# A two-layer GNN on one core: early zeros, and a packed copy of layer 1's edge rows

## The chip, the cores and the metric

The kernel runs on one core of a Trainium2 chip. The metric is the device time of one execution in microseconds (us). Engines are named as in the profile: PE (TensorE), DVE (VectorE), ACT (ScalarE), POOL (GpSimd) and SP (SyncE, which here only issues DMAs). Each engine runs its own program in order, and they meet at semaphores.

## The reference

There are 6250 nodes and 206250 edges (100000 random pairs in both directions, and a self loop each), sorted by destination. Both layers take the same edges. Cut to what matters:

```
for layer, attr, kd in ((0, edge_attr_16, 16), (1, edge_attr_64, 64)):
    h = relu(layernorm(x))                       # 6250 x 64
    if layer == 0:
        ea  = attr @ W_edge.T + b_edge
        agg = segment_sum(relu(h[src] + ea), dst)
        g   = (h + agg) @ W1.T + b1
        g   = relu(batch_norm(g, gamma, beta)) @ W2.T + b2
    else:
        y   = relu(concat(h[src], attr) @ M_W.T + M_b)
        z   = segment_sum(y, dst)
        g   = relu(concat(h, z) @ U_W.T + U_b)
    x = x + g
```

## The kernel before

The edges are cut into 34 groups (NB) of 31 tiles of 128 edges whose order is changed, and 16 "plain" tiles, and a 35th part of plain tiles alone. A turn works on one group. Layer 0 has 33 turns after a first group, and so has layer 1. Two sets of buffers alternate.

**The edge store.** PE projects the attributes of an edge for both layers at once (line 1128), ACT takes the results out of PSUM (lines 862 and 865) into a staging row of 132 floats (528 B), and POOL scatters the rows of one tile of 128 edges to their slots in DRAM with one indirect DMA (line 732). A group has 6400 slots (50 columns of 128), sorted by source node. The first 66 floats of a row are layer 0's half, those from 64 on are layer 1's half (they share two floats of metadata). Slots that no edge takes must be zero, so `fill` (line 523) writes 3300 KB of zeros before a group is scattered, three groups ahead of its use. Layer 0 reads its half of a group with `load_edges` (line 527), layer 1 reads the other half with `load_edges_part` (line 532) in two parts; both take one run of 264 B from each row: 6400 runs in a group, 4096 and 2304 in the two parts.

**A turn.** Edges of a group are met with node rows by one-hot matmuls on PE (lines 1163, 1181), added and passed through relu on DVE and ACT (lines 1600, 907), and summed by destination in a window with another one-hot matmul (line 1193; DVE line 1591 makes the one-hot). Layer 0 also makes the one-hot matrix of the sources (DVE 1576) and SP stores it (line 546, `store_src`), from where layer 1 loads it on ACT's queue (line 912). For plain tiles POOL gathers node rows with 16 indirect DMAs in a turn (line 754), in both layers.

**The order of the work** is written out by hand: every engine's program is a loop over turns, with two turns in its body. SP's in layer 0 is `turn`, which walks over u = 0 to 6: `store_src` at each, `next_edges` (line 527) at u = 1, attributes (line 473) at u = 2, 4, 5, 6, the zeros of the group three ahead at u = 3, plain indices at u = 4; then attributes of the next plain tiles and the plain rows (line 515). A DMA that waits for a semaphore holds up all that follow it on SP. POOL scatters 16 tiles, later 15, and gathers 16 in one turn of layer 0. In layer 1 `turn_l1` issues indices, the two parts of an edge load two groups ahead, and plain rows (line 519).

**Before the loops** SP issues attributes for group 0, the zeros of group 0, indices, the rest of group 0's attributes, x, four attribute loads of group 1, the zeros of group 1, and so on (lines 586 to 627). `load_first` from the third on waits for a projection. DVE makes layernorm steps (lines 1405 to 1442) and POOL's slot indices (line 1531), and adds b2 to x (line 1772) ahead of the first group. At the end of each layer every engine waits for a flag and loads it into a register (line 460, in `if_general`), to decide whether a general path for unusual graphs is needed; it isn't with these inputs.

Of the kernel before, what the change touches and what calls it, by code (L numbers as in the profile page):

```python
# [212 lines left out]
def build(nc, x, idx, dst, attr0, attr1, params, out):  # L213
# [4 lines left out]
    store_groups = store.rearrange("(g r) c -> g r c", r=GROUP_ROWS)  # L218
    plain_store = nc.dram_tensor("plain_store", (PARTS, P, PLAIN * D), F32, kind="Internal").ap()
    src_store = nc.dram_tensor("src_store", (NB, NODE_P, NODE_COLS * P), BF16, kind="Internal").ap()  # L220
    with ExitStack() as ctx:
# [185 lines left out]
        rows_landed = [[sem(f"rows_landed{s}_{v}") for v in range(NV)] for s in range(2)]  # L407
        plain_projected = sem("plain_projected")
# [48 lines left out]
        def if_general(eng, general):  # L457

            eng.wait_ge(windows_ready, 1)
            more = eng.value_load(flag_int[0:1, 0:1], min_val=0, max_val=1)  # L460
            with eng.If(more > 0):
                general()
                eng.nop()
            with eng.Else():
                eng.nop()
            eng.nop()

        @block.sync
        def _(sp):
# [60 lines left out]
            def load_edges_part(g, p, k):  # L530
                j, nj = LOAD_PARTS[k]
                sp.dma_start(edge[p][:, j:j + nj, :], store_groups[bass.ds(g, 1), 0:CAP * NODE_COLS, D:D + HALF_ROW]
                             .rearrange("a (p j) c -> p (a j) c", j=NODE_COLS)[:, j:j + nj, :]).then_inc(dense_sems[1].e_landed[p], 16)
# [53 lines left out]
            sp.dma_start(dst_all[:, 0:head], dst[:, 0:head]).then_inc(head_landed, 16)  # L587
            for quarter in range(2):
                load_first(0, quarter)
            sp.wait_ge(memsets_done, 1)  # L590
            fill(0, 0)
# [8 lines left out]
            for quarter in range(NQ):  # L600
                load_first(1, quarter)
            fill(1, 1)
            sp.wait_ge(filled[0], 16)
# [21 lines left out]
            for u in range(NU):  # L625
                store_src(0, 0, u)

# [7 lines left out]
            def turn(n, s, more=True, more_fill=True):  # L635

                m = n * 2 + s
                for u in range(NU):
                    store_src(m + 1, 1 - s, u)
                    if u == 1 and not (isinstance(m, int) and m + 2 >= NB):  # L640
                        next_edges(m, s)
                    if more and u in (2, 4, 5, 6):
                        load(m, (2, 4, 5, 6).index(u) + 2)
                    if u == 4:
                        next_plain_idx(0, n, s)
                    if u == 3 and more and more_fill:
# [16 lines left out]
            if_general(sp, lambda: general(0))  # L663

            sp.wait_ge(dense_sems[0].rows_used, NB * NU + 2)
            for g in range(2):
                for k in range(2):
                    load_edges_part(g, g, k)
# [45 lines left out]
            if_general(sp, lambda: general(1))  # L714
# [7 lines left out]
        def _(pool):  # L722
# [61 lines left out]
            if_general(pool, lambda: general(0))  # L784
# [14 lines left out]
            if_general(pool, lambda: general(1))  # L799

        @block.scalar
        def _(act):
# [235 lines left out]
            for m in range(LAST_PREPARED, NB - 1):  # L1038
                dense_turn(0, m // 2, m % 2, more=m <= LAST_PREPARED, last=m == NB - 2, bank=0)
            for m in range(NB - 1, PARTS):  # L1040
                last_plain(0, m)
            last_windows(0)
            if_general(act, lambda: general(0))
# [30 lines left out]
            for m in range(NB - 4, NB - 1):  # L1074
                dense_turn(1, m // 2, m % 2, last=m == NB - 2)
            for m in range(NB - 1, PARTS):
                last_plain(1, m)
            last_windows(1)
            if_general(act, lambda: general(1))

        @block.tensor
        def _(pe):
# [263 lines left out]
            for m in range(LAST_PREPARED + 1, NB - 1):  # L1346
                dense_turn(0, m // 2, m % 2, last=m == NB - 2, bank=0)
            for m in range(NB - 1, PARTS):
                last_plain(0, m)
            last_windows(0)  # L1350
            if_general(pe, lambda: general(0))
# [25 lines left out]
            dense_turn(1, (NB - 2) // 2, 0, last=True)  # L1377
            for m in range(NB - 1, PARTS):
                last_plain(1, m)
            last_windows(1)  # L1380
            if_general(pe, lambda: general(1))
# [10 lines left out]
        def _(dve):  # L1392
# [356 lines left out]
            for step in range(NG + 3):  # L1749
# [17 lines left out]
                if step == 5:  # L1767
# [18 lines left out]
            for m in range(LAST_PREPARED + 1, NB - 1):  # L1786
                dense_turn(0, m // 2, m % 2, last=m == NB - 2)
            for m in range(NB - 1, PARTS):
                last_plain(0, m)
            last_windows(0)  # L1790
            if_general(dve, lambda: general(0))
# [52 lines left out]
            dense_turn(1, (NB - 2) // 2, 0, last=True)  # L1844
            for m in range(NB - 1, PARTS):
                last_plain(1, m)
            last_windows(1)
            if_general(dve, lambda: general(1))
# [76 lines left out]
```

## Time and profile before

| | us |
|---|---|
| median of 3 runs | 4705.78 |
| lowest, highest | 4699.32, 4708.74 |
| profiled execution | 4683.44 |
| its span, first to last instruction | 4681.6 |
| POOL busy, instructions | 2085.3, 2185 |
| PE busy, instructions | 2569.9, 25733 |
| mean granted clock of PE, share of full speed | 0.673 |

Busy time is time in which an engine runs an instruction; registers, branches and DMA issues don't count. In a timeline a row gives start, length, what ran, and in brackets how long the engine was idle before and what released it: "issue" means that it waited for nothing that the profile shows, "remote" or "an unknown queue" that the releaser is not known. A "q" after an engine's name is its sequencer. For SP the length of a row of several issues reaches from the first to the last.

### The profile page before, as it was taken

How to read it: one execution, taken by the hardware profiler on the slowest of the kernel's cores; microseconds unless marked ns; L12 is line 12 of the kernel's file. 1: busy time of each engine (PE TensorE's matmuls, PEld its weight loads, DVE VectorE, ACT ScalarE, POOL GpSimd, SP SyncE). 2: the span in 40 equal slices, each digit the busy share in tenths (PEclk: the TensorE clock that was granted, in tenths of full speed). 3: DMA queues.
4: the chain of work that ended last, by engine and by line, in shares of the span. 5: the costliest groups of instructions: out<-in, count | busy, mean ns of one | idle time of the engine just before them, and what ended most of it. 6: DMA issues, size and time to landing. Idle time of an engine off the chain costs nothing. (4 is left out here: it accounts for less than half of the span.)

```text
span 4681.6 us, 73575 instructions
## 1 busy us (share of the span) xinstructions
PE 2569.9 (55%) x25733; PEld 2124.4 (45%) x25733; DVE 1518.7 (32%) x2605; ACT 961.3 (21%) x2153; POOL 2085.3 (45%) x2185
## 2 busy tenths in 40 slices
PE   3455546554655556555456554655655545555554
PEld 3454445444544445444445444544544434443443
DVE  4422223222332223322232222322444434433443
ACT  1322212211221112221122221212321111111111
POOL 4444444455345543454434444354244443444343
PEclk9766667666666666766666666666667666666676
DMA  6554435443444434544345444443355555555552
GB/s 191 142 140 124 114 106 144 135 116 106 123 132 135 112 105 123 136 132 113 106 129 141 118 113 112 123 118 81 93 123 126 122 120 116 125 121 121 115 123 55
DMA packets 703632, 565.17 MB, mean 121 GB/s; under 512 B 491942, under 2 KB 605748, under 8 KB 699042
## 3 DMA queue, kind: packets, MB, share of 16 engines
q1 hardware_dynamic: 625244, 402.10, 34.3%
q0 software_dynamic: 69440, 107.94, 9.1%
q10 hardware_dynamic: 8736, 51.91, 3.2%
q8 instruction: 180, 2.95, 0.3%
q14 instruction: 32, 0.26, 0.0%
HBM read 294.89 MB, written 266.88 MB: 120 GB/s over the span
## 5 line engine op out<-in xcount | busy, mean ns | idle before, releaser
L1193 PE MATMUL ps_w<-arena 128*64 128x128 f32 (+1 forms) x9040 | 1209.1, 313 | 1031.1 <-issue 942.3
L732 POOL DMA_INDIRECT edge_store<-side,slot_idx x1054 | 1018.3, 966 | 1544.0 <-issue 1244.5
L754 POOL DMA_INDIRECT gathered_rows<-node_table_l,plain_slot x1116 | 1059.2, 949 | 957.9 <-DVE arena L1614 573.1
L1193 PEld LDWEIGHTS ps_w<-arena 128*64 128x64 f32 x9040 | 898.8, 165 | 1235.4 <-issue 1119.5
L1591 DVE TENSOR_TENSOR arena<-ps_c,dst_rel 128x1024 f32<-128x1024 f32 (+1 forms) x476 | 526.1, 1105 | 1186.4 <-remote 890.6
L907 ACT ACTIVATE arena<-arena 128x512 f32<-128x512 f32 (+1 forms) x616 | 366.2, 595 | 2369.3 <-remote 887.3
L1128 PE MATMUL ps_p<-w_both,side 80*128 80x128 f32 x3228 | 647.1, 362 | 368.1 <-issue 109.6
L1128 PEld LDWEIGHTS ps_p<-w_both,side 80*128 80x128 f32 x3228 | 565.4, 262 | 419.4 <-issue 245.5
L1600 DVE TENSOR_TENSOR arena<-ps_r,arena 128x512 f32<-128x512 f32 (+1 forms) x476 | 299.4, 629 | 586.0 <-remote 562.8
L1576 DVE TENSOR_SCALAR arena<-arena,iota_p 125x512 bf16<-125x512 bf16 (+1 forms) x442 | 147.5, 351 | 940.7 <-ACT arena L894 538.6
L1181 PE MATMUL ps_r<-tab,arena 125*128 125x64 bf16 x5100 | 287.6, 213 | 251.2 <-issue 132.7
L1181 PEld LDWEIGHTS ps_r<-tab,arena 125*128 125x128 bf16 x5100 | 238.8, 111 | 324.6 <-issue 248.7
L894 ACT ACTIVATE arena<-ps_b 125x512 bf16<-125x512 f32 (+1 forms) x442 | 244.2, 575 | 520.7 <-remote 474.2
L862 ACT ACTIVATE side<-ps_p 128x512 f32<-128x512 f32 (+1 forms) x272 | 156.9, 577 | 516.0 <-remote 346.5
L1181 PE MATMUL ps_r<-tab,ranking 125*128 125x64 bf16 x2550 | 139.0, 209 | 166.7 <-issue 161.1
L1163 PE MATMUL ps_b<-ident_b,marks_b 128*125 128x128 bf16 x1700 | 214.9, 263 | 22.1 <-ACT dst_rel L888 17.0
L1181 PE MATMUL ps_r<-tab,side 125*128 125x64 bf16 x2550 | 135.4, 206 | 156.0 <-issue 155.7
L1181 PEld LDWEIGHTS ps_r<-tab,ranking 125*128 125x128 bf16 x2550 | 107.9, 108 | 208.9 <-issue 201.1
L1181 PEld LDWEIGHTS ps_r<-tab,side 125*128 125x128 bf16 x2550 | 104.9, 106 | 195.2 <-issue 189.1
L1163 PEld LDWEIGHTS ps_b<-ident_b,marks_b 128*125 128x125 bf16 x1700 | 168.9, 171 | 24.5 <-issue 23.1
L1591 DVE TENSOR_TENSOR arena<-ps_c,plain_rel 128x576 f32<-128x576 f32 x140 | 105.2, 752 | 52.2 <-remote 38.1
L874 ACT ACTIVATE plain_e<-ps_p 128x512 f32<-128x512 f32 x140 | 79.9, 592 | 192.4 <-remote 145.6
(124 smaller groups left out, 1026.3 us busy)
## 6 DMA issues: line engine op xcount, KB each, us to landing
edge_store<-zeros SPq DMA_DIRECT2D x34, 3300.0 KB
arena<-edge_store SPq DMA_DIRECT2D x34, 1650.0 KB
src_store<-arena SPq DMA_DIRECT2D x204, 250.0 KB
side<-attr SPq DMA_DIRECT2D x172, 256.0 KB
arena<-edge_store SPq DMA_DIRECT2D x34, 1056.0 KB
arena<-edge_store SPq DMA_DIRECT2D x34, 594.0 KB
plain_store<-plain_e SPq DMA_DIRECT2D x35, 512.0 KB
side<-plain_store SPq DMA_DIRECT2D x35, 512.0 KB
```

The lines of the kernel that those rows point to most:

```text
L732: pool.indirect_dma_start(out=store, in_=stage[:, c, i, :], in_offset=None, out_offset=bass.IndirectOffsetOnAxis(ap=slot_idx[:, s, t + i:t ...
L754: pool.indirect_dma_start(out=rows[s][:, i, :], out_offset=None, in_=table[layer], in_offset=bass.IndirectOffsetOnAxis(ap=plain_slot[:, s, ...
L862: act.activation(stage[:, c, 0:nt, :].rearrange("p t (l r) -> p t l r", l=2)[:, :, :, 0:D], ps_p[(s + 1 + c) % 2][:, 0:nt * P].rearrange(" ...
L894: act.activation(spread_src[0:NODE_P, (p + i // 2) % 2, i % 2, 0:nt * P], ps_b[(p + i) % 2][0:NODE_P, 0:nt * P], ACT.Copy).then_inc(copied, 1)
L907: act.activation(msg[:, slot, 0:nt, :], pre[:, slot, 0:nt, :], ACT.Relu).then_inc(d.relu_done, 1)
L1128: last = pe.matmul(ps_p[bank][:, i * P:(i + 1) * P], attr_buf[:, slot, e:e + P], w_both[:, :], start=True, stop=True)
L1163: last = pe.matmul(ps_b[(p + i) % 2][0:NODE_P, t * P:(t + 1) * P], marks_b[:, p, j + t:j + t + 1].broadcast_to([P, NODE_P]), ident_b[:, :] ...
L1181: last = pe.matmul(ps_r[slot][:, to:to + D], match, tab[:, j + t, k, :], start=(k == 0), stop=(k == 2))
L1193: mm = pe.matmul(ps_sum[layer][t % 2][:, 0:width], msg[:, slot, t, :], dst_match[:, slot, t, 0:width], start=(first and t <= layer), stop= ...
L1576: dve.tensor_scalar(src_match[0:NODE_P, slot, i % 2, 0:nt * P], spread_src[0:NODE_P, slot, i % 2, 0:nt * P], iota_p[0:NODE_P, 1:2], None, ...
L1591: dve.tensor_tensor(dst_match[:, slot, 0:nt, 0:width], iota[:, 0:width].unsqueeze(1).broadcast_to([P, nt, width]), rel.unsqueeze(2).broadc ...
L1600: dve.tensor_tensor(pre[:, slot, 0:nt, :], ps_r[(p + u) % 2][:, 0:nt * D].rearrange("p (t d) -> p t d", d=D), edge[p][:, j:j + nt, at:at + ...
```

## The change

- A second DRAM tensor, `e1_store`, holds layer 1's half of every row of a group side by side, per partition. In each turn of layer 0 for which group m + 2 exists, SP copies that half from `edge_store` with one DRAM to DRAM DMA, at u = 5 behind the attribute load; groups 0 and 1 are copied before the first turn. Layer 1 waits once for all copies and loads from there: per partition one run of 8448 B and one of 4752 B.
- In the prologue the zeros of group 0 go before the first attribute loads, and those of group 1 after two instead of four attribute loads of that group.
- DVE's addition of b2 moves from before the first group to after the first two turns.
- PE, ACT and DVE load the flag before their last plain units instead of after them. SP and POOL load it where they did.

```diff
+    e1_store = nc.dram_tensor("e1_store", (NB, P, NODE_COLS * HALF_ROW), F32, kind="Internal").ap()
...
-        def if_general(eng, general):
-
+        def general_flag(eng):
             eng.wait_ge(windows_ready, 1)
-            more = eng.value_load(flag_int[0:1, 0:1], min_val=0, max_val=1)
+            return eng.value_load(flag_int[0:1, 0:1], min_val=0, max_val=1)
+
+        def if_general(eng, more, general):
+
             with eng.If(more > 0):
...
             def load_edges_part(g, p, k):
                 j, nj = LOAD_PARTS[k]
-                sp.dma_start(edge[p][:, j:j + nj, :], store_groups[bass.ds(g, 1), 0:CAP * NODE_COLS, D:D + HALF_ROW]
-                             .rearrange("a (p j) c -> p (a j) c", j=NODE_COLS)[:, j:j + nj, :]).then_inc(dense_sems[1].e_landed[p], 16)
+                sp.dma_start(edge[p][:, j:j + nj, :].rearrange("p j c -> p (j c)"),
+                             e1_store[bass.ds(g, 1), :, j * HALF_ROW:(j + nj) * HALF_ROW].rearrange("a p c -> (a p) c"))\
+                    .then_inc(dense_sems[1].e_landed[p], 16)
+
+            def pack_e1(g):
+
+                sp.dma_start(e1_store[bass.ds(g, 1)].rearrange("a p (j c) -> p (a j) c", c=HALF_ROW),
+                             store_groups[bass.ds(g, 1), 0:CAP * NODE_COLS, D:D + HALF_ROW]
+                             .rearrange("a (p j) c -> p (a j) c", j=NODE_COLS)).then_inc(e1_packed, 16)
...
+            sp.wait_ge(memsets_done, 1)
+            fill(0, 0)
             for quarter in range(2):
                 load_first(0, quarter)
-            sp.wait_ge(memsets_done, 1)
-            fill(0, 0)
...
-            for quarter in range(NQ):
+            for quarter in range(2):
                 load_first(1, quarter)
             fill(1, 1)
+            for quarter in range(2, NQ):
+                load_first(1, quarter)
...
             for u in range(NU):
                 store_src(0, 0, u)
+            for g in range(2):
+                pack_e1(g)
...
                     if u == 4:
                         next_plain_idx(0, n, s)
+                    if u == 5 and not (isinstance(m, int) and m + 2 >= NB):
+                        pack_e1(m + 2)
...
             sp.wait_ge(dense_sems[0].rows_used, NB * NU + 2)
+            sp.wait_ge(e1_packed, NB * 16)
             for g in range(2):
                 for k in range(2):
                     load_edges_part(g, g, k)
...
+            more = general_flag(act)
             for m in range(NB - 1, PARTS):
                 last_plain(0, m)
             last_windows(0)
-            if_general(act, lambda: general(0))
+            if_general(act, more, lambda: general(0))
...
-            dve.wait_ge(centred[0], NG)
-            dve.tensor_tensor(xs[:, :, :], xs[:, :, :],
-                              prm("b2", NODE_P).unsqueeze(1).broadcast_to([NODE_P, NODE_COLS, D]), ALU.add)\
-                .then_inc(b2_added, 1)
...
             for s in range(2):
                 dense_turn(0, 0, s, more=True, first=s == 0)
+            dve.wait_ge(centred[0], NG)
+            dve.tensor_tensor(xs[:, :, :], xs[:, :, :],
+                              prm("b2", NODE_P).unsqueeze(1).broadcast_to([NODE_P, NODE_COLS, D]), ALU.add)\
+                .then_inc(b2_added, 1)
```

The flag's lines stand alike for both layers and for PE and DVE.

## Rows read from the trace of the kernel before

**Rows 1.** The page, part 1: busy time and share of each engine.

```profile
PE 2569.9 (55%) x25733; PEld 2124.4 (45%) x25733; DVE 1518.7 (32%) x2605; ACT 961.3 (21%) x2153; POOL 2085.3 (45%) x2185
```

**Rows 2.** Timeline of POOL, a turn of layer 0: start, length, what, [idle <- releaser].

```profile
1882.54 1.00 POOL L732 DMA_INDIRECT edge_store<-side,slot_idx  x1 [31.55 <-issue]
...
1908.88 0.96 POOL L732 DMA_INDIRECT edge_store<-side,slot_idx  x1 [6.34 <-ACT side L865]
```

**Rows 3.** Timeline of PE in the same turn, columns as before.

```profile
1925.95 0.46 PE L1193 MATMUL ps_w<-arena 128*64 128x128 f32 x1 [1.04 <-issue]
...
1953.30 3.78 PE L1128 MATMUL ps_p<-w_both,side 80*128 80x128 f32 x16 [5.29 <-ACT plain_e L874]
```

**Rows 4.** Windows of that turn: busy PE, PEld, DVE, ACT, POOL; PEclk, DMA share, GB/s.

```profile
1867.00:1877.00 10.00, 7.04 (x121) 6.30 (x118) 9.57 (x22) 4.11 (x10) 0.00 (x0) 1.00 1.04 204
1881.00:1897.00 16.00, 8.18 (x78) 6.46 (x76) 3.26 (x7) 2.40 (x6) 11.11 (x12) 0.89 0.95 296
...
1912.00:1947.00 35.00, 12.82 (x68) 8.84 (x67) 1.85 (x3) 2.11 (x6) 26.47 (x29) 0.60 0.19 48
```

**Rows 5.** Windows of layer 1, same columns; the last three are turns.

```profile
3912.00:3932.00 20.00, 6.69 (x87) 4.43 (x83) 3.60 (x5) 2.00 (x5) 15.12 (x16) 0.64 0.61 158
4581.00:4596.00 15.00, 12.51 (x187) 10.78 (x188) 10.62 (x15) 3.77 (x8) 0.00 (x0) 0.70 0.01 2
4488.20:4525.20 37.00, 20.49 (x293) 15.73 (x289) 14.63 (x21) 6.11 (x14) 15.13 (x17) 0.68 0.52 120
4525.20:4560.80 35.60, 18.61 (x292) 14.89 (x289) 14.48 (x21) 6.04 (x14) 15.10 (x17) 0.71 0.55 117
...
4596.90:4631.00 34.10, 19.44 (x276) 14.49 (x272) 14.42 (x21) 6.12 (x14) 15.12 (x16) 0.70 0.14 32
```

**Rows 6.** Chain of waits of layer 1: start, length, what.

```profile
4490.32 3.54 another core or an unknown queue
4493.94 16.92 another core or an unknown queue
```

**Rows 7.** Timeline of SP (its DMA issues), turns of layer 0.

```profile
1867.13 0.63 SPq L527 DMA_DIRECT2D arena<-edge_store  x1
1870.09 5.28 SPq L546 DMA_DIRECT2D src_store<-arena  x1
...
1907.97 1.06 SPq L473 DMA_DIRECT2D side<-attr  x2
...
1920.13 38.77 SPq L473 DMA_DIRECT2D side<-attr  x6
...
1965.25 0.64 SPq L527 DMA_DIRECT2D arena<-edge_store  x1
```

**Rows 8.** Timeline of SP in a turn of layer 1.

```profile
3905.34 18.83 SPq L532 DMA_DIRECT2D arena<-edge_store  x2
```

**Rows 9.** Line 532, issue ns min/median/max, first and last start.

```profile
L532 SPq DMA_DIRECT2D arena<-edge_store x68: 378/384/17404, 3345.6 to 4559.2; - x68
```

**Rows 10.** Timeline of POOL in the prologue.

```profile
85.98 0.96 POOL L732 DMA_INDIRECT edge_store<-side,slot_idx  x1 [26.69 <-DMA edge_store<-zeros]
...
132.59 0.96 POOL L732 DMA_INDIRECT edge_store<-side,slot_idx  x1 [5.90 <-ACT side L865]
```

**Rows 11.** Timeline of SP in the prologue.

```profile
42.39 0.87 SPq L473 DMA_DIRECT2D side<-attr  x2
...
68.25 4.28 SPq L473 DMA_DIRECT2D side<-attr  x4
72.57 6.73 SPq L523 DMA_DIRECT2D edge_store<-zeros  x2
```

**Rows 12.** Timeline of DVE in the prologue.

```profile
116.04 1.77 DVE L1517 TENSOR_TENSOR ranking<-ps_p,ranking 128x1550 f32<-128x1550 f32 x1 [9.70 <-remote]
...
154.48 3.49 DVE L1772 TENSOR_TENSOR xs<-xs,par 125x3200 f32<-125x3200 f32 x1
```

**Rows 13.** Timeline of DVE between the layers.

```profile
3353.27 3.00 DVE L1797 BATCH_NORM_STATS2 bn<-acc 64x6 f32<-64x500 f32 x5 [1.20 <-DVEq L1792]
```

More of the change, by code:

```diff
@@ L407, in build @@
         rows_landed = [[sem(f"rows_landed{s}_{v}") for v in range(NV)] for s in range(2)]
+        e1_packed = sem("e1_packed")
         plain_projected = sem("plain_projected")
@@ L662, in _ @@
                 store_plain(m)
-            if_general(sp, lambda: general(0))
+            if_general(sp, general_flag(sp), lambda: general(0))
             sp.wait_ge(dense_sems[0].rows_used, NB * NU + 2)
+            sp.wait_ge(e1_packed, NB * 16)
             for g in range(2):
@@ L713, in _ @@
                 turn_l1(m // 2, m % 2, more=m < NB - 3)
-            if_general(sp, lambda: general(1))
+            if_general(sp, general_flag(sp), lambda: general(1))
             for g, (j, m) in enumerate(GROUPS):
@@ L782, in general @@
                             ).then_inc(e.rows_landed, 16)
-            if_general(pool, lambda: general(0))
+            if_general(pool, general_flag(pool), lambda: general(0))
             pool.wait_ge(turned[0], NG)
@@ L798, in _ @@
             gather_plain(1, NB // 2, 0)
-            if_general(pool, lambda: general(1))
+            if_general(pool, general_flag(pool), lambda: general(1))
         @block.scalar
@@ L1075, in _ @@
                 dense_turn(1, m // 2, m % 2, last=m == NB - 2)
+            more = general_flag(act)
             for m in range(NB - 1, PARTS):
@@ L1078, in _ @@
             last_windows(1)
-            if_general(act, lambda: general(1))
+            if_general(act, more, lambda: general(1))
         @block.tensor
@@ L1347, in _ @@
                 dense_turn(0, m // 2, m % 2, last=m == NB - 2, bank=0)
+            more = general_flag(pe)
             for m in range(NB - 1, PARTS):
@@ L1350, in _ @@
             last_windows(0)
-            if_general(pe, lambda: general(0))
+            if_general(pe, more, lambda: general(0))
             pe.wait_ge(sums_done[0], 1)
@@ L1377, in _ @@
             dense_turn(1, (NB - 2) // 2, 0, last=True)
+            more = general_flag(pe)
             for m in range(NB - 1, PARTS):
@@ L1380, in _ @@
             last_windows(1)
-            if_general(pe, lambda: general(1))
+            if_general(pe, more, lambda: general(1))
             pe.wait_ge(sums_done[1], 1)
@@ L1787, in _ @@
                 dense_turn(0, m // 2, m % 2, last=m == NB - 2)
+            more = general_flag(dve)
             for m in range(NB - 1, PARTS):
@@ L1790, in _ @@
             last_windows(0)
-            if_general(dve, lambda: general(0))
+            if_general(dve, more, lambda: general(0))
             dve.drain().then_inc(sums_done[0], 1)
@@ L1844, in _ @@
             dense_turn(1, (NB - 2) // 2, 0, last=True)
+            more = general_flag(dve)
             for m in range(NB - 1, PARTS):
@@ L1847, in _ @@
             last_windows(1)
-            if_general(dve, lambda: general(1))
+            if_general(dve, more, lambda: general(1))
             dve.drain().then_inc(sums_done[1], 1)
```

## The prediction

> **What bounds the kernel now.** The page comes first: no engine is over 55% busy [rows 1], so busy time bounds nothing and the waits must be read. I then read the timelines of one turn of each layer, the windows that cut the turn where POOL works, and last the prologue and the seam between the layers.
>
> In layer 0 a turn has two bursts of indirect DMAs on POOL, from 1882.54 and from 1908.88 [rows 2]. Some 12 us after the second begins, PE, which had work, starts one matmul at a time with 1 to 3 us of "issue" before each (1925.95 is one of 14 such rows), until the burst ends near 1947.6 [rows 3]. It did 68 matmuls in 35 us, most of these in the first 10. The DMA engines were only 0.19 busy meanwhile [rows 4], so PE does not crawl because data is late; it crawls while POOL issues. POOL itself keeps its pace whatever the queues carry: 12 instructions in 16 us with the burst begun 1.5 us into it (14.5/12 = 1.21 us each) at a DMA share of 0.95, and 35/29 = 1.21 us each at 0.19 [rows 4].
>
> In layer 1 the same is seen. In 20 us with POOL busy PE issues 87 matmuls, in 15 us without it 187 [rows 5]. The chain of waits names an unknown releaser for 3.54 + 16.92 us of one turn of 37 us [rows 6], exactly this crawl. So each of the 33 turns of layer 1 is about 20 us of burst plus 16 us of dense work, and each of the 33 of layer 0 (98.1 us between two edge loads [rows 7]) is set by two bursts and the work between. What the change touches, the edge load of layer 1, stands in neither part as a releaser.
>
> **The change part by part.**
>
> *Layer 1's loads* (32 turns with loads). The two issues hold SP for 18.83 us in one turn [rows 8], 17.40 at worst for one of them [rows 9]; with 128 runs each instead of 4096 and 2304 that shrinks. Behind them on SP stand the load of plain rows and the indices, and neither is a releaser in any turn I looked at. The case gives its own control: the last load is issued at 4559.2 [rows 9], so the turn from 4596.90 has none. It takes 34.10 us against 35.60 for a turn with them (and 37.00 for another), with 276 matmuls where they have 292 and 293 [rows 5]; it also lacks ACT's loads of one-hot data. Upper bound 1.5 us a turn, 32 x 1.5 = 48 us; lower bound 0. The no-load turn lacks 16 matmuls too, and its burst part crawls like the others, so I take a value near the lower end: 0.2 us a turn, -6 us.
>
> *The packs in the turns* (32). SP issues each right after the attribute load at 1907.97 [rows 7], and DMA share after 1912 is 0.19 for 35 us [rows 4]. Nearest row: the edge load of layer 0 reads as many runs of 264 B in the 10 us from 1867 at a share of 1.04 [rows 4, 7]. The pack reads as much and writes as much: from 10 us, if both sides overlap, to 20 if they add up, to some 40 if runs written to DRAM cost three times those read. What is queued behind it: one store of one-hot data, on which SP may hang as it did for 5.28 us at 1870.09 behind the edge load, then the attribute loads from 1920.13 [rows 7], whose data PE takes at 1953.30 [rows 3]. That is 33 us from issue; less 6 that I allow for the transfer, 27 of slack. A pack of 15 us is over at 1925. I charge 0. POOL's pace did not feel a full queue, and layer 0's own edge load and fill come in the next turn after 1963, 50 us later. Without this cover every microsecond past it would count 32 times.
>
> The page "DMA: Bandwidth & Descriptors" of the Trainium skill, under "Specifications", says that under 512 B a transfer leaves line rate and becomes a read-modify-write. It speaks against this change, which adds 34 x 6400 such writes. No row before has a plain DMA writing 264 B to DRAM. By the rule the pack comes out at the upper values of the range above; while it is under 37 us that changes nothing. The same page's "Issuing engines are not separate DMA queues" says all share 16 engines, so that scatters and pack interleave; the rows agree only in that POOL's pace was 1.21 us either way [rows 4].
>
> *The two first packs* lie on the queue before turn 0, ahead of the load of group 2 and of attributes. 2 x 10 to 2 x 20 us of transfers once, beside the dense start of layer 0: 0 to +10 us; I take +1, since the first loads of attributes are kept three groups ahead.
>
> *Early zeros.* POOL's second scatter burst starts at 85.98 after 26.69 us idle, released by the zeros [rows 10]. These were issued at 72.57, behind four attribute loads of which the third and fourth wait from 43 to 68.25 for projections [rows 11]. The change puts the fill (3300 KB, 11 us at the 296 GB/s of [rows 4]) at about 43.3, so it lands by 55. Then POOL can start when DVE gives the slots, about 68.5: 17.5 us earlier. That is no gain by itself, for PE then crawls in 80 to 109 instead of 91 to 126. What follows is the layernorm chain on DVE, which does not need POOL; it stands 9.70 us before 116.04 because PE crawls [rows 12], and only that can come back. POOL's third burst begins at 132.59, after ACT [rows 10]. So the gain lies between 0 and 9.7 us, 17.5 if all of the chain moved; it may be -3 (a loss) as the first fill now stands ahead of the first attribute loads. I take -6.
>
> *The flag* is loaded before the last plain units instead of in the chain: DVE's 1.20 us before 3353.27 contain it [rows 13], about 0.6 us of it goes, twice: -1 us. *b2*: 3.49 us of DVE [rows 12] leave a place with idle time behind it and come back once between turns 1 and 2, where DVE is under a third busy: 0 to +3.5, I take +1.
>
> **Sum.** -6 (loads) + 0 + 1 (packs) - 6 (zeros) - 1 (flag) + 1 (b2) = -11 us. The profiled execution took 4683.4 us (span 4681.6 and 1.8 around it): 4672.4. The runs shown have their median 22.3 us higher, 4705.8, so I forecast 4694.8, 0.23% less. About 0.2% (9.4 us) is what a measurement can tell from no change, so the forecast sits at the border.
>
> **The rivals.**
>
> *Layer 1 gets shorter.* If the many short packets are what delays PE in part, the turns fall to the no-load turn: -48 - 5 = -53 us, 4653. For it: 34.10 against 35.60 and PE's 276 matmuls in less time. Against: the missing ACT loads, the 16 missing matmuls, and the crawl at a DMA share of 0.19 in layer 0. The whole crawl going (16.92 us a turn) I hold for near impossible.
>
> *Slower: a pack that outlasts its cover.* Place: the queue behind 1909 in layer 0; price: 32 us for each microsecond by which the attribute data come after 1953. It decides from a pack of about 37 us (1909.6 + 37 = 1946.6, plus 6 for the load). At 40 us, +3 x 32 = +96: 4791 with the rest of the sum. A milder form, in which scatters and pack interleave and a turn gets 0.5 us longer, gives +16: 4711. For it: ends of the cost are far apart and no row shows the writes. Against: 27 us of slack, and POOL's indifference.
>
> *Nothing shows.* The zeros only move the crawl and the loads were hidden: -1 us at most, 4704.
>
> **How the numbers follow.** Forecast case 0.60 (its own range 4680 to 4711; 0.36 faster by over 0.2%, 0.24 within); layer 1 shorter 0.12; nothing 0.12; slower 0.16, half of it mild. Faster 0.48, same 0.36, slower 0.16. The range reaches from the layer 1 rival's value up beyond the mild pack: 4653 to 4722.
>
> **What would show it.** Right: the window of layer 1's bursts again near 87 matmuls in 20 us and turns of 35.5 to 37 us, though SP's issues of line 532 are short; DMA share in the second burst of layer 0 up from 0.19 to about 0.5 for 15 us and the turn still about 98 us; POOL's second burst at about 69 and the first turn's start some 6 us earlier. Wrong: PE or ACT in layer 0 waiting for attributes (a releaser "side<-attr") after 1953; layer 1 turns at 34 us; a first turn that starts no earlier, or later, than before.

## The result and the profile after

The changed kernel takes 4738.57 us (median of 5 runs, 4728.07 to 4748.14) against 4705.78: a ratio of 1.0069, 95% interval 1.0044 to 1.0094. It is 33 us slower, where 11 us faster was forecast. The profiled execution of the changed kernel has a span of 4746.3 us, 65 us above the one before. The profiled execution of before lies 22 us under its median and that of the changed kernel 10 us over its own, so of the 65 some 32 are the two executions'. One of five executions of the kernel before in this measurement took 5070.88 us and does not enter the ratio.

First the page (busy time; DMA share in 40 slices; the hardware queue's packets, MB and the time its packets took as a share of 16 engines' span), with the queue's line of before last:

```profile
PE 2588.9 (55%) x25733; PEld 2153.1 (45%) x25733; DVE 1515.9 (32%) x2605; ACT 960.8 (20%) x2153; POOL 2087.8 (44%) x2185
...
DMA  6676777677767676666766677565544344344341
...
q1 hardware_dynamic: 634492, 459.55, 45.5%
```

```profile
q1 hardware_dynamic: 625244, 402.10, 34.3%
```

Busy time of the engines hardly moves, while the hardware queue goes from 402.10 MB and 34.3% to 459.55 MB and 45.5%, and in layer 0 the DMA engines are 0.6 to 0.7 busy where they were mostly at 0.4. Packets added and time added give the price of a copy, below.

Where the 65 us arise is read from POOL's timeline, for POOL has two bursts a turn and its rows line up one by one in the two traces. These are the rows of the prologue's second and third burst and of the first burst of turn 0 (start, length, what, idle before):

```profile
71.38 0.96 POOL L751 DMA_INDIRECT edge_store<-side,slot_idx  x1 [10.25 <-ACT side L884]
...
132.76 0.96 POOL L751 DMA_INDIRECT edge_store<-side,slot_idx  x1 [18.02 <-ACT side L884]
...
280.82 1.00 POOL L751 DMA_INDIRECT edge_store<-side,slot_idx  x1 [82.72 <-issue]
```

The second burst starts 14.6 us earlier than in [rows 10], the third at 132.76 against 132.59: nothing left. The first burst of turn 0 starts at 280.82; before, it started at 241.83:

```profile
241.83 1.00 POOL L732 DMA_INDIRECT edge_store<-side,slot_idx  x1 [44.96 <-issue]
```

The burst between these two starts at 158.15 before and at 159.38 after, so nearly all of the 39 us is lost between 159 and 281, once. From there to the first burst after layer 0 the traces differ by 27 us more (3169.5 us before, 3196.7 after, over 33 turns; much of it is scatter between executions, as the crawling chip shows below), and through layer 1 by -1 us (1219.7 and 1218.6).

The 39 us are seen on SP's timeline, on the chain of waits and on DVE's timeline:

```profile
171.12 49.83 SPq L557 DMA_DIRECT2D src_store<-arena  x7
221.00 14.40 SPq L542 DMA_DIRECT2D e_store<-edge_store  x2
235.86 18.91 SPq L557 DMA_DIRECT2D src_store<-arena  x2
255.85 0.67 SPq L531 DMA_DIRECT2D arena<-edge_store  x1
```

```profile
221.62 13.78 SPq L542
235.86 27.95 DMA src_store<-arena
```

```profile
263.90 0.62 DVE L1599 TENSOR_SCALAR arena<-arena,iota_p 125x512 bf16<-125x512 bf16 x2 [30.78 <-DMA src_store<-arena]
```

SP hangs in the issue of the second of the two first copies for 13.78 us (line 542), and the one-hot store behind them (line 557) lands late: DVE, which needs the buffer that this store frees, waits 30.78 us for it, and the chain runs 27.95 us through the DMA. POOL's slot indices come from DVE too, and its burst follows. Before the change the edge load that stands behind the two stores was issued at 226.59, now at 255.85. The windows show how full the DMA engines are meanwhile (first row a stretch before turn 0 in the trace of before, second row the copies, the others layer 1 after the change; columns as in [rows 4]):

```profile
200.00:241.00 41.00, 32.66 (x448) 30.06 (x449) 30.64 (x57) 18.89 (x38) 0.00 (x0) 0.87 0.40 96
```

```profile
221.00:262.00 41.00, 9.01 (x123) 7.86 (x121) 7.23 (x13) 5.50 (x11) 0.00 (x0) 0.69 1.27 97
4015.70:4051.10 35.40, 19.69 (x294) 15.61 (x291) 14.63 (x21) 6.15 (x15) 15.16 (x17) 0.71 0.43 125
4051.10:4087.40 36.30, 20.47 (x291) 15.46 (x287) 14.48 (x21) 6.04 (x14) 15.11 (x16) 0.67 0.39 117
4660.80:4696.10 35.30, 19.38 (x274) 15.37 (x270) 14.45 (x21) 6.06 (x14) 15.11 (x16) 0.71 0.14 31
```

In 41 us after 221 PE does 123 matmuls where it did 448. The share is 1.27 with POOL at rest, at 97 GB/s only; a share above 1 says that packets' times overlap on an engine. The two copies, 3.4 MB read and written again, fill nearly all of that stretch: about 20 us each.

### The profile page after: what moved, and what is told of

Its sections match the earlier page's. It is cut to its first block, busy times and chain, and to the rows that moved or that the text cites. A ratio compares the mean times of both kernels' runs of the same rounds, so it can differ in the third digit from the quotient of the medians.

```text
span 4746.3 us, 73700 instructions
## 1 busy us (share of the span) xinstructions
PE 2588.9 (55%) x25733; PEld 2153.1 (45%) x25733; DVE 1515.9 (32%) x2605; ACT 960.8 (20%) x2153; POOL 2087.8 (44%) x2185
## 3 DMA queue, kind: packets, MB, share of 16 engines
q1 hardware_dynamic: 634492, 459.55, 45.5%
q0 software_dynamic: 69440, 107.94, 11.3%
## 4 chain that ended last, share of the span: by engine, by line
another core or an unknown queue 35%; PE 32%; issue 17%; DVE 7%; ACT 3%; DMA 2%; SPq 1%; DVEq 1%; ACTq 0%; POOL 0%; POOLq 0%
PE ps_w L1214 14%; PE ps_p L1149 9%; PE ps_r L1202 5%; DVE arena L1614 2%; DMA src_store<-arena 2%; PE ps_b L1184 2%; DVE arena L1623 1%; DVE ranking L1540 1%; SPq L557 1%; ACT arena L926 1%; PE ps_p L1141 1%; DVE arena L1637 1%; ACT arena L913 1%; DVEq L1605 1%
## 5 line engine op out<-in xcount | busy, mean ns | idle before, releaser
L1214 PE MATMUL ps_w<-arena 128*64 128x128 f32 (+1 forms) x9040 | 1228.8, 315 | 1053.4 <-issue 966.2
L1214 PEld LDWEIGHTS ps_w<-arena 128*64 128x64 f32 x9040 | 919.4, 167 | 1259.9 <-issue 1161.1
L1149 PE MATMUL ps_p<-w_both,side 80*128 80x128 f32 x3228 | 658.4, 366 | 421.5 <-ACT side L884 112.7
L1149 PEld LDWEIGHTS ps_p<-w_both,side 80*128 80x128 f32 x3228 | 575.9, 267 | 470.6 <-issue 266.4
L1202 PEld LDWEIGHTS ps_r<-tab,side 125*128 125x128 bf16 x2550 | 101.8, 105 | 131.7 <-issue 128.2
```

What stands on the lines that cost most here:

```text
L1149: last = pe.matmul(ps_p[bank][:, i * P:(i + 1) * P], attr_buf[:, slot, e:e + P], w_both[:, :], start=True, stop=True)
L1202: last = pe.matmul(ps_r[slot][:, to:to + D], match, tab[:, j + t, k, :], start=(k == 0), stop=(k == 2))
L1214: mm = pe.matmul(ps_sum[layer][t % 2][:, 0:width], msg[:, slot, t, :], dst_match[:, slot, t, 0:width], start=(first and t <= layer), stop= ...
```

## The experiments

Kernels were measured in groups, each group on one chip beside the kernel before. **The chips differ.** On the chip of the result, and on one that ran three of the experiments (it may be the same), the kernel before takes about 4700 us, and PE crawls under POOL's bursts. On four others the same kernel takes 3053 to 3055 us and PE doesn't crawl. I call them the crawling and the free chips. What makes the difference isn't known; it was not chosen. It gave the study its control.

How the free chip looks, from c_zeros_only, which is the kernel before but for two fills: a window of 20 us inside a burst of 32 gathers in layer 1:

```profile
2234.00:2254.00 20.00, 18.30 (x368) 15.96 (x366) 17.52 (x24) 7.68 (x17) 15.23 (x16) 0.89 0.99 188
```

PE does 368 matmuls in 20 us with POOL at work, against 87 in [rows 5]. The granted clock, 0.89 here and 0.64 there, accounts for a factor of 1.4 of the 4.2 at most.

### Free chips

**a_late_first.** The first two copies stand behind layer 0's loop:

```diff
-            for g in range(2):
-                pack_e1(g)
...
+            for g in range(2):
+                pack_e1(g)
             if_general(sp, general_flag(sp), lambda: general(0))
```

> The changed kernel with the copies of groups 0 and 1 moved from before the first turn to after layer 0's loop. Theory 1 (these two transfers sit on SP's queue ahead of the stores of one-hot data that DVE waits for, and POOL's burst of the first turn came at 280.8 instead of 241.8): 39 us come back, about 4700, and that burst starts near 242. Theory 2 (each copy in a turn costs about 1 us and that is the whole loss): within 5 us of the changed kernel's 4738. Theory 3 (the early zeros shift the prologue): the burst still starts near 280.

Measured: 3559.36 us against 3052.81, ratio 1.1674 (1.165 to 1.1698). No expectation was for such a chip. It lost 507 us, so copies in the turns are dear here.

**b_packs_only.** The kernel before with `pack_e1` at u = 5 and two copies behind the loop, old loads in layer 1.

> The kernel before with the 32 copies in the turns and the two first copies after layer 0's loop; layer 1 loads as before, no other edit. Theory 1 (a copy in a turn is nearly hidden; layer 0's turns after the first drifted by 28 us over 31 turns in the profiles): +15 to +30 us over before. Rival (that drift is scatter between executions): within 5 us of before.

Measured: 3635.05 us, ratio 1.1915 (1.1891 to 1.1939), so +582 us. On the same chip a_late_first, which has long loads in layer 1 (and the early zeros and the flag besides), takes 76 us less. Repeated on another free chip (b_packs_only_4 below) it was 3538.40, 1.1579, so the same kernel differs by 97 us between two free chips, and the 76 holds for the one chip.

**c_zeros_only.**

```diff
+            sp.wait_ge(memsets_done, 1)
+            fill(0, 0)
             for quarter in range(2):
                 load_first(0, quarter)
-            sp.wait_ge(memsets_done, 1)
-            fill(0, 0)
...
-            for quarter in range(NQ):
+            for quarter in range(2):
                 load_first(1, quarter)
             fill(1, 1)
+            for quarter in range(2, NQ):
+                load_first(1, quarter)
```

> The kernel before with the early zeros alone. Theory (POOL's second burst starts some 15 us earlier, but the third stays at 132.6, set by the layernorm chain on DVE and ACT): within 2 us of before. Rival (my forecast): 6 us faster.

Measured: 3058.43 us, ratio 1.0017 (1.0008 to 1.0027). Early zeros gain nothing; they lose some 5 us.

**e_long_copy.** The copy's two sides are contiguous per partition:

```diff
-                sp.dma_start(e1_store[bass.ds(g, 1)].rearrange("a p (j c) -> p (a j) c", c=HALF_ROW),
-                             store_groups[bass.ds(g, 1), 0:CAP * NODE_COLS, D:D + HALF_ROW]
-                             .rearrange("a (p j) c -> p (a j) c", j=NODE_COLS)).then_inc(e1_packed, 16)
+                sp.dma_start(e1_store[bass.ds(g, 1)].rearrange("a p c -> (a p) c"),
+                             store_groups[bass.ds(g, 1), 0:CAP * NODE_COLS // 2, :]
+                             .rearrange("a (p j) c -> (a p) (j c)", j=NODE_COLS // 2)).then_inc(e1_packed, 16)
```

> As b_packs_only, but each copy moves the same number of bytes (1650 KB) of the group's first rows in long runs (13.2 KB per partition) instead of 6400 runs of 264 B; what it stores isn't used. Theory (the copy lasts about 20 us because of its short runs): it lasts under 12 us, and whatever b_packs_only loses is halved or gone. Rival (the bytes through DRAM cost, not the runs): same length of about 20 us and the same loss.

Measured: 3060.59 us, ratio 1.0016 (1.0004 to 1.0028). The same bytes in long runs cost 8 us in all (5 by the ratio), and in short runs 582. So it is the runs, not the bytes.

The pages of the three kernels (span; DMA share in slices; the hardware queue q1; for two of them POOL's queue q0), first c_zeros_only, then b_packs_only, then e_long_copy:

```profile
span 3060.3 us, 73575 instructions
...
DMA  8767767766876776687677668644576868777771
...
q1 hardware_dynamic: 625244, 402.10, 52.1%
q0 software_dynamic: 69440, 107.94, 13.8%
```

```profile
span 3626.2 us, 73700 instructions
...
DMA  7899989899988889988899888889696777777772
...
q1 hardware_dynamic: 843388, 459.55, 63.3%
q0 software_dynamic: 69440, 107.94, 16.4%
```

```profile
q1 hardware_dynamic: 626876, 459.55, 57.6%
```

The queue's share times span times 16 engines gives packet time: 0.521 x 3060.3 = 1594 us of all engines without copies, 0.633 x 3626.2 = 2295 us with them, 0.576 x 3061.8 = 1764 us with long ones. Over 34 copies that is 20.6 us for a copy in short runs and 5.0 us for one in long runs. b_packs_only has 218144 packets more, 6400 and a few for each copy, and 51 ns of one engine for each.

The time of a packet also holds what it waits for others: POOL's queue has the same 69440 packets in both kernels, and they take 422 us of all engines without copies and 595 with them. So 20.6 us is what a copy adds to the hardware queue in this company. Other runs with 34 such copies give 18.0 us (b_packs_only_4) and 21.7 us (d_packs_u6) against the same c_zeros_only; the figure is good to 2 or 3 us. In i_first_two_only, with just two copies one behind the other, the median from issue to landing is 33.9 us, which 22 or 23 us for each would give (an estimate: one lands after 23, the other after 45).

And this is what the copy does to a turn. SP's timeline, c_zeros_only and then b_packs_only, from one edge load (line 527 or 529) to the next:

```profile
1002.28 0.65 SPq L527 DMA_DIRECT2D arena<-edge_store  x1
...
1040.85 8.79 SPq L473 DMA_DIRECT2D side<-attr  x6
...
1062.41 0.64 SPq L527 DMA_DIRECT2D arena<-edge_store  x1
```

```profile
1009.93 0.63 SPq L529 DMA_DIRECT2D arena<-edge_store  x1
...
1044.65 0.56 SPq L539 DMA_DIRECT2D e_store<-edge_store  x1
1046.90 23.24 SPq L554 DMA_DIRECT2D src_store<-arena  x1
1070.47 11.77 SPq L475 DMA_DIRECT2D side<-attr  x6
...
1088.66 0.64 SPq L529 DMA_DIRECT2D arena<-edge_store  x1
```

A turn is 60.1 us without and 78.7 us with the copy. The copy is issued at 1044.65; the store of one-hot data behind it hangs 23.24 us at its issue, and the attribute loads, 38.6 us after the edge load without the copy, are issued 60.5 us after it. PE then waits for them (line, waits in total, times, longest), c_zeros_only and b_packs_only:

```profile
PE ps_p L1130 <- DMA side<-attr: 329.7, 34, 13.7
```

```profile
PE ps_p L1141 <- DMA side<-attr: 893.2, 68, 21.2
```

563 us more of waiting for attributes, where the kernel is 582 us slower. A turn is 60 us here and 98 us on the crawling chip, so 38 us of cover are gone, and this is the slower rival of the prediction, in its place and with its releaser. It is not the whole cause: d_packs_u6 below takes this wait away and keeps the loss.

**after_again.** The changed kernel itself.

> The changed kernel itself, unchanged, beside the kernel before. The runs so far were on a chip on which the kernel before takes 3053 us and PE does not crawl through most of a POOL burst. If this chip is like that one: Theory 1 (copies of short runs fill the DMA engines, which bound layer 0 there, and long loads give about 75 us back in layer 1): 3590 us, 40 us over a_late_first's 3559 for the two first copies. If it is like the first one: 0.7% over before.

Measured: 3597.02 us, ratio 1.1802 (1.1756 to 1.1849), as the first theory had it (3590). The same change that costs 0.7% on one chip costs 18% on another.

**f_l1_short_loads.** `j, nj = LOAD_PARTS[k][0], 1`: 128 runs in each part.

> The kernel before, with each of layer 1's edge loads cut to one column (128 runs of 264 B instead of 4096 and 2304); the rest of the rows is left out, so it bounds what any layout of layer 1's edge rows can give. Theory for a chip with the crawl (before near 4700): turns of layer 1 keep 35 to 37 us, under 0.5% of the time. For a chip without it (before near 3050): turns of layer 1 shorten from 49 us per two gathers of 16 by 2 us or more per turn, 75 to 150 us in all, since a_late_first had 76 us less than b_packs_only.

Measured: 2912.97 us, ratio 0.954 (0.9524 to 0.9556); repeated as f_short_loads_4: 2919.09, 0.9551. Layer 1's edge loads are worth at most 141 us on a free chip, 4.4 us a turn. The copies of b_packs_only cost four times that.

**g_l1_half_gathers.** `range(v * UNIT, v * UNIT + nt, 2 if layer else 1)` for POOL's gathers, and half the counts.

> The kernel before with every second of POOL's plain gathers of layer 1 left out (8 instead of 16 in a turn). Theory (PE crawls while POOL issues indirect DMAs): on a chip with the crawl a turn of layer 1 loses about 10 of its 36 us, 330 us in all. Rival (the crawl is from the other DMAs): under 3 us a turn. On a chip without the crawl: under 5 us a turn unless POOL's issues bound layer 1.

Measured: 3006.61 us, ratio 0.9849 (0.9833 to 0.9866); repeated as g_half_gathers_4: 3002.94, 0.9826. 1.5 us a turn: on a free chip POOL's issues don't set layer 1. On the crawling chip it wasn't tried.

**d_packs_u6.** As b_packs_only with `u == 6` for `u == 5`.

> As b_packs_only, with the copy issued one step later in a turn (at u = 6, behind the store of one-hot data and the attribute load that it stood ahead of). Theory 1 (a copy costs because of what stands behind it on SP's queue, one-hot stores and attributes): at least a third of b_packs_only's loss goes. Theory 2 (a copy costs by the DMA engines' time, wherever it stands): the loss stays within a tenth of b_packs_only's (19% of the time on the chip without the crawl).

Measured: 3599.86 us, ratio 1.1798 (1.1764 to 1.1832). Of b_packs_only's 19% this is 94%, but on another chip, and b_packs_only itself was 15.8% on a third. So no third of the loss goes by moving the copy behind the attribute load. The waits of its trace say why (the first line is DVE's wait for a one-hot store; it is 377.3 us in c_zeros_only and 322.7 in b_packs_only):

```profile
DVE arena L1589 <- DMA src_store<-arena: 716.7, 65, 19.1
...
PE ps_p L1141 <- DMA side<-attr: 338.6, 35, 12.1
```

PE's wait for attributes is back at what it was without copies (329.7), and 339 us of waiting for stores have come in its place (the three traces are of two free chips). Whatever stands behind the copy waits: on a free chip it is the copy's time on the DMA engines that costs, and its place on the queue only chooses who shows it. The second theory holds roughly; its tenth can't be told across chips.

**i_first_two_only.** The kernel before with the two first copies alone.

```diff
             for u in range(NU):
                 store_src(0, 0, u)
+            for g in range(2):
+                pack_e1(g)
```

> The kernel before with the copies of groups 0 and 1 alone, before the first turn; no copies in the turns, layer 1 loads as before. Theory 1 (on either kind of chip each copy holds the 16 DMA engines for about 20 us, and nothing before the first turn hides the two): 39 us over before. Rival (what came late in the first turn was the early zeros' doing): within 5 us.

Measured: 3085.08 us against 3055.04, ratio 1.0103 (1.0086 to 1.012): 30 us, for two copies.

**l_rows_528.** The copy moves whole rows, `store_groups[bass.ds(g, 1), 0:CAP * NODE_COLS, :]`, to rows with a pitch of 560 B.

> As b_packs_only, but a copy moves whole rows of 528 B, from contiguous rows to rows with a pitch of 560 B, so 6400 runs of 528 B and twice the bytes; what it stores isn't used. Rule under test (writes under 512 B are the dear ones): a copy takes no longer than with 264 B, near 20 us, and the loss is that of b_packs_only or less although the bytes double. Rival (time per run grows with its bytes): 25 us or more a copy, and more loss than b_packs_only, over 700 us on a chip without the crawl.

Measured: 3575.12 us, ratio 1.1702 (1.1677 to 1.1727): a loss between the two of b_packs_only (15.8% and 19.2% on two other chips), with double the bytes. Its span and queue:

```profile
span 3579.4 us, 73700 instructions
...
q1 hardware_dynamic: 843388, 517.00, 64.1%
```

0.641 x 3579.4 = 2294 us, as much as b_packs_only's 2295 and 700 over c_zeros_only: 20.6 us a copy, 51 ns a run, for 528 B as for 264 B, within the 18.0 to 21.7 us that copies of 264 B show. The rival of a price that grows with the bytes is out for packet time. (From issue to landing these copies take 28.6 us in the median; the page of b_packs_only has no such figure to set beside it.) In GB/s a copy ran at 82 with runs of 264 B, at 164 with 528 B and at 338 in long runs. Two readings remain: a price per run that doesn't know its bytes, or a surcharge below 512 B that happens to match. The read side alone isn't the price: layer 0's edge load, 6400 runs of 264 B into SBUF, takes 10 us [rows 4, 7], half of a copy. Whether the other half is the writing of short runs to DRAM wasn't shown; no run has short runs on one side of a copy only.

**a_late_first_2** and **h_flag_b2** (the flag's and b2's lines of the diff alone):

> a_late_first once more, to have it on the kind of chip that the result came from, if this is one. With the crawl (before near 4700): the two first copies are 39 of the 33 to 65 us that the change lost, so within 10 us of before plus what copies in the turns cost, 4700 to 4725. Without the crawl: 3559 as before.

> The kernel before with only the flag's load put ahead of the last plain units on PE, ACT and DVE, and b2 added after the first two turns. Theory: 1 to 2 us faster, too little to tell from none. Rival: b2 delays the third turn by its 3.5 us, so 2 us slower.

Measured: 3554.26 us, ratio 1.1628, as before on another free chip; and 3055.30, ratio 1.0004 (0.9993 to 1.0014), nothing.

### The crawling chip

> On a chip with the crawl (before near 4700): Theory 1 (the two first copies cost 39 us of the change's loss, and those in the turns 0.5 to 1 us each): 4700 to 4725. Theory 2 (the loss lies in the turns): 4730 or more. On a chip without it: 3555 as before, nothing new.

> The kernel before with the copies of groups 0 and 1 alone. With the crawl: Theory 1: 39 us over before, POOL's first burst of turn 0 near 280 instead of 242. Rival (the crawl hides them, the early zeros delayed the turn): within 5 us. Without it: 30 us over, as measured.

> As b_packs_only, with the copy in every second turn alone (16 of 32) and the two first ones behind the loop. Theory (each copy adds its DMA time to a turn whose DMA engines are the bound): half of the loss of b_packs_only, 290 us on a chip without the crawl, 5 to 15 us on one with it. Rival (a turn without a copy catches up on one with it): under a third, less than 190 us.

The edit of n_half_copies is `u == 5 and s == 0`. The kernel before took 4695.96 us here (20 runs, 4670.19 to 4709.85).

| kernel | median us | ratio (95%) |
|---|---|---|
| a_late_first_3 | 4703.24 | 1.0020 (0.9997 to 1.0044) |
| i_first_two_3 | 4726.26 | 1.0087 (1.0058 to 1.0117) |
| n_half_copies | 4710.13 | 1.0036 (1.0015 to 1.0057) |

The two first copies alone cost 0.87%, as much as the whole change (0.69%, intervals overlap). With them behind the loop the change with all its 32 other copies is at 0.20%, not told from none. POOL's rows for the third burst and the first of turn 0 show it, a_late_first_3 and then i_first_two_3:

```profile
132.87 0.96 POOL L751 DMA_INDIRECT edge_store<-side,slot_idx  x1 [19.45 <-ACT side L884]
...
246.52 1.00 POOL L751 DMA_INDIRECT edge_store<-side,slot_idx  x1 [47.74 <-issue]
```

```profile
131.86 0.96 POOL L743 DMA_INDIRECT edge_store<-side,slot_idx  x1 [5.30 <-ACT side L876]
...
275.10 1.00 POOL L743 DMA_INDIRECT edge_store<-side,slot_idx  x1 [79.64 <-issue]
```

246.52 against 241.83 before, and 275.10 with the two copies alone. The first theory holds in both. Its 39 us come out as 30 in the medians (41 by the ratio, whose interval is 27 to 55) and as 29 to 34 in the bursts. The cleanest pair is 280.82 against 246.52: the changed kernel with the copies in the one place and in the other.

The copies in the turns are nearly hidden: +7 us for 32 of them with long loads behind, +14 for 16 of them with old loads, intervals of some 10 us either side. Part of both isn't the turns': the two copies behind the loop now stand ahead of layer 1's loads. From the statistics at the end of layer 0 (DVE's BATCH_NORM_STATS2) to POOL's third burst of layer 1 the traces have 128.9 us before, 129.3 in i_first_two_3 and 131.7 after the change, but 136.3 in a_late_first_3 and 137.5 in n_half_copies, so some 5 to 9 us arise there. In the turns of layer 0, from turn 0's first burst to those statistics, the traces have 3111.4 us before and 3101.4 in i_first_two_3 (no copies in turns), 3125.8 in n_half_copies (16), 3115.6 in a_late_first_3 and 3138.4 after the change (32 each). Two executions with equal turns differ by 10 and by 23 us, so a cost of 0 to 1 us a copy is all that can be said (an estimate from these rows and the medians). This doesn't grow with their number as far as can be told; n_half_copies' question stays open here.

> The kernel before with every second of POOL's plain gathers of layer 1 left out (8 instead of 16 in a turn). On a chip with the crawl (before near 4700): Theory (PE crawls while POOL issues indirect DMAs, so a turn is POOL's burst plus PE's dense work): a burst of 10 instead of 20 us, 8 to 10 us less in each of 33 turns, 260 to 330 us in all, with the rest of the turn unchanged. Rival (POOL's bursts are only there when PE crawls for another reason): under 3 us a turn. Without the crawl: 3007 as before.

> The kernel before with layer 1's edge loads cut to one column (128 runs of 264 B instead of 4096 and 2304), the rest of the rows left out: the bound of what any layout can give. With the crawl: Theory (the loads lie under POOL's burst): at most 0.2 to 1 us a turn, 5 to 30 us. Rival (the loads help to make the crawl): 1.5 us a turn or more, over 45 us. Without it: 2913 as before.

> Copies in the turns and two behind the loop, layer 1 loads as before. With the crawl: Theory (the 32 copies in the turns cost under 1 us each, and long loads in layer 1 give nothing): 10 to 30 us over before and within 10 us of a_late_first_3. Without it: 3635 as before.

These three met a free chip again; their numbers stand above. What layer 1's loads are worth on the crawling chip, and whether halving POOL's gathers shortens its turns, stays without a run.

## Why the prediction was wrong

**The step that failed** is "*The two first packs* lie on the queue before turn 0 ... 0 to +10 us; I take +1, since the first loads of attributes are kept three groups ahead". They cost 39 us in the profile of the changed kernel and 30 alone (i_first_two_3). The length of a copy was only a part of the mistake: some 20 us lies in the range of 10 to 40 that I had for it, and even its low end, 2 x 10 us, is more than the +1 that I took, so the step rests on the copies being hidden. The mistake was the look for who stands behind them. I looked at the attributes only. Behind the copies on SP's queue stand the one-hot stores, and each store frees a buffer for which DVE waits (30.78 us at 263.90); PE and POOL's next burst then wait for DVE. That a store hangs was in my rows (5.28 us at 1870.09 in [rows 7]), and I used it for the turns, where a burst of POOL covers it, but not before turn 0, where POOL stands still for 44.96 us between its bursts in the trace of before and PE works densely (448 matmuls in 41 us), so that little is covered. With 39 for that term the sum is -12 + 39 = +27 us, and the result is +33. That this comes near is in part luck: the runs leave 27 to 55 us for the term, and two others below are open by several us each.

**Copies in the turns: 0.** Right on the crawling chip within some 10 us (a_late_first_3), for the reason given in most turns. SP's timeline of a turn after the change, and the windows of POOL's burst in it:

```profile
1952.49 1.07 SPq L477 DMA_DIRECT2D side<-attr  x2
1954.06 0.35 SPq L542 DMA_DIRECT2D e_store<-edge_store  x1
1954.83 14.83 SPq L557 DMA_DIRECT2D src_store<-arena  x1
1971.35 31.83 SPq L477 DMA_DIRECT2D side<-attr  x6
```

```profile
1953.00:1963.00 10.00, 8.57 (x60) 7.69 (x59) 2.58 (x4) 1.46 (x4) 7.56 (x9) 0.82 1.13 138
1963.00:1990.00 27.00, 5.66 (x18) 3.70 (x19) 0.00 (x0) 0.59 (x2) 20.60 (x22) 0.51 0.81 96
```

The store behind the copy hangs 14.83 us; the attribute loads are issued from 1971.35, 18.9 us after those at u = 5 against 12.2 before [rows 7], and POOL's burst lasts until 1991, with PE still crawling. A share of 0.5 for 15 us was forecast for the burst; it is 1.13 for 10 us and 0.81 for 27 more, so the copy seems longer than the 15 us that I reckoned with. The 27 us of slack were enough in most turns, not in all. PE's waits for attributes, before and after:

```profile
PE ps_p L1128 <- DMA side<-attr: 5.4, 2, 4.9
```

```profile
PE ps_p L1149 <- DMA side<-attr: 35.3, 9, 8.7
```

This is the sign of being wrong that the prediction named, on a small scale: seven waits more, 30 us in all, and 68.8 us in 13 waits in a_late_first_3. Most stand before 16 matmuls like those of 1953.30 in [rows 3], which waited 5.29 us for ACT there, so only a part of them need be lost time. The mild form of the slower rival, 0.5 us a turn, isn't ruled out. On the free chips there is no such slack, and the kernel is 16 to 19% slower, as the slower rival has it. I had its place, queue and releaser, and put its start at a copy of 37 us; with a turn of 60 us in place of 98 it starts below the 20 us that a copy takes.

**Early zeros: -6.** Nothing of it is seen: POOL's third burst gained nothing. The burst does start 14.6 us earlier (17.5 was forecast). DVE's stall of 9.70 us [rows 12] doesn't vanish, it splits:

```profile
110.38 0.20 DVE L1447 RECIPROCAL ln_inv<-ln_std 125x8 f32<-125x8 f32 x1 [5.10 <-issue]
...
116.25 1.77 DVE L1540 TENSOR_TENSOR ranking<-ps_p,ranking 128x1550 f32<-128x1550 f32 x1 [3.00 <-remote]
```

5.10 + 3.00 us, and the slots of group 2 are at 116.25 against 116.04. The crawl follows the burst. The gain lies at the low end of my 0 to 9.7, not at the 6 that I took. By themselves the early zeros ran only on a free chip, where they cost some 5 us (c_zeros_only, ratio 1.0008 to 1.0027).

**Layer 1's loads: -6.** Right in size as far as the traces tell; no run on the crawling chip has the long loads alone. From POOL's third burst of layer 1 to its last the traces with the old loads have 1148.8 us (before), 1151.0 (i_first_two_3) and 1157.2 (n_half_copies), those with long loads 1145.2 (after) and 1143.9 (a_late_first_3): 4 to 13 us less. SP's longest issue fell from 17.40 us to 0.77:

```profile
L536 SPq DMA_DIRECT2D arena<-e_store x68: 328/333/774, 3412.4 to 4622.9; - x68
```

and that moved little, since turns are still 35.4 and 36.3 us, and the one without loads 35.3 us, where the turn of before without loads had 34.10 [rows 5]. So the 1.5 us a turn that I held for a possible gain is no more than turns differ among themselves. On a free chip the loads are worth up to 4.4 us a turn.

**The flag and b2.** DVE's idle time before the statistics fell from 1.20 us to 0.56, as forecast; both are too small for any run to show.

**The price of short runs and the shared engines.** The rule of the Trainium skill's page "DMA: Bandwidth & Descriptors", "Specifications", that under 512 B a transfer leaves line rate, warned rightly of this change: in long runs the same bytes went four times as fast (5.0 us against 20.6). But the runs don't show the boundary at 512 B: a run of 528 B took the same 51 ns as one of 264 B, and 528 B in that time is half the rate of long runs. The same page of the Trainium skill says under "Issuing engines are not separate DMA queues" that DMAs of all issuing engines run on the same 16 DMA engines and interleave. The free chips agree: POOL's 69440 packets take 422 us of all engines without copies on SP's queue and 595 us with them.

## What to carry to other kernels

When a transfer is put on a queue, list every DMA behind it and, for each, who waits for it: a store counts too when it frees a buffer. Do this for each place where it is issued; cover found in the steady turn doesn't hold for the start. Here a copy within DRAM cost by the run, so repacking short runs pays 6400 runs once more before the reader saves any, and here the reader's saving was at most 4.4 us a turn (on a free chip) for 20.6 us of DMA time. And moving the copy on its queue changes who waits for it; where the DMA engines have no idle time left it doesn't change the price.

## What the runs showed of the hardware

The same kernel takes 4700 us on one kind of chip and 3055 us on four chips of another. The difference that the traces show is PE under POOL's bursts: 87 matmuls in 20 us against 368, at a granted clock of 0.64 and 0.89. Why isn't known. POOL's own pace is the same 1.25 us for a DMA on both. A change's price depends on it: 0.7% on one kind, 18% on the other. A copy from DRAM to DRAM in 6400 runs added 20.6 us of packet time on all 16 DMA engines whether a run had 264 or 528 B (18.0 to 21.7 us over the runs), and 5.0 us in long runs. Behind such a copy SP hung in its next issue, for 13.78 us before turn 0, 14.83 us in a turn on the crawling chip and 23.24 us on a free one.
